# A gated delta-rule layer with experts: weights loaded in parts, biases added on VectorE, and sums of squares taken by ScalarE from transposed tiles

## The chip, the cores and the metric

The kernel runs on one core of a Trainium2 chip. The metric is the device time of one execution in microseconds (us), lower is better. A core has TensorE (PE; its weight loads are PEld), VectorE (DVE), ScalarE (ACT), GpSimd (POOL) and SyncE (SP), which issues the DMAs. Each engine runs its own instructions in the order in which the program gives them; semaphores join the engines.

## The reference, cut to what matters

Two batches of 2048 tokens with 256 features pass a gated delta-rule attention with a short convolution, and then a layer of one shared and 16 routed experts. The sums of squares in question are those of `_l2norm`; the biases in question are `bz`, `bb` and `ba`.

```python
mixed = hidden_states @ Wqkv.T + bqkv
z = hidden_states @ Wz.T + bz
beta = sigmoid(hidden_states @ Wb.T + bb)
a = hidden_states @ Wa.T + ba
g = -exp(A_log) * softplus(a + dt_bias)
mixed = silu(causal_conv4(mixed))              # then split into q, k (8 heads), v (16 heads)
q = _l2norm(q) * DK ** (-0.5);  k = _l2norm(k) # x * rsqrt(sum(x*x) + 1e-6)
# per token: state = state*exp(g); delta = (v - k.state)*beta; state += k delta; out = q.state
core = out * rsqrt(mean(out*out) + 1e-6) * norm_w * silu(z)
x = x + layernorm(core @ Wout.T + bout)
# then x = x + layernorm(shared expert + routed experts of layernorm(x))
```

## The kernel before, in words

The tokens are cut into 32 chunks of 128. The 16 value heads of a chunk are four groups, and one item `(t, g)` is one group of one chunk: 128 items. The recurrence within a chunk is solved by blocks: a triangular matrix is inverted, in part by GpSimd (16x16 blocks) and in part by matmuls.

Work is pipelined over items. When item `w` is in its state stage (`s`), item `w+1` (called `v`) is inverted (`i`), item `w+2` (`f`) is in its front stage, item `w+3` (`a`) is projected, and the output of item `w-1` (`u`) is projected (`p`). Between them stand the experts of the chunk before (`e`) and the norm and gates of the chunk after (`c`). Every engine has one function `item(w, stages)` in which this order is written out by hand, and `run` calls it for a few items ahead of the loop (the prologue), for the loop over chunks 1 to 30 (`Fori`, four items in one pass), and behind it. Nothing reorders the instructions.

The steps that the change and the prediction touch:

- **Loads.** SyncE issues the broadcast rows, then all weights, and every engine waits for all of them (`loaded`). VectorE then prepares constants: it scales `Wout` by `norm_w` (L1069), and splits `bz` and `bb, ba` into three bf16 parts each (L1077 to L1084), so that a bf16 matmul can add them.
- **Projection.** `proj` (PE L450) makes the q, k and v channels of item `a` as 128x128 tiles in the banks bF0 and bF1, with channels on partitions. ACT applies the last convolution tap (L810), VectorE the other three (L1101), and `activated` runs Silu to QK, Gz and VT. Two table loads (L793) stand around the Silus.
- **Gate.** `z_proj` adds `bz` by a bf16 matmul of 512 columns (L459), then makes z (L460, L462) in bF1. ACT takes Silu from the bank straight to Gz (L831). `chunk_front("ba")` has such a bias matmul too (L630).
- **Sums of squares.** ACT squares QK as one 128x512 instruction (L826, at the end of `activated`); `ss` has PE multiply each of the four squared tiles with a column of ones (L477), because channels lie on partitions; VectorE adds epsilon (`squares`, L1136), and ACT makes the logarithm and the inverse scale (`key_norm`, L844). `ktr` transposes the two k tiles (L484) into the bank bXT, which `ss` used too, and so waits for L1136. GpSimd's `exponents` (from L1444) starts at the logarithm and makes Parts, which `parts_t` transposes (L490).
- **Front and state.** `kkq` (L469) makes the products of keys and queries; `correct` (L565) and `refined` (DVE L1151) finish the inverse Tt; `right_side` (DVE L1158) and `solve` (L587) use it.

## Time and profile before

| | |
|---|---|
| median of three runs | 3621.46 us (3620.43 to 3624.41) |
| the profiled execution | 3620.91 us, of which the span is 3619.1 us |
| PE | 3296.9 us busy, 91% |
| DVE | 2712.9 us, 75% |
| ACT | 2441.7 us, 67% |
| POOL | 2162.0 us, 60% |
| mean granted clock of TensorE | 0.966 of full speed |

The busy shares are averages over the whole span, in which the first 68 us and the last 100 us look unlike the rest. Matmuls overlap, so the duration of one is longer than the distance from one to the next: where the text speaks of what a matmul costs, it means the distance between starts. A float32 matmul of the program appears as two records, a transpose as one. Records of some matmuls are missing in the loop (those of L459 and L502, for instance); a gap called "issue" of some 0.2 us stands in their place.

### The profile page before, as it was taken

To read this page: it belongs to the slowest core of one execution; us is meant where nothing else is said; L and a number is where in the kernel's file an instruction comes from. 1 tells how busy PE (TensorE), PEld (TensorE's weight loads), DVE (VectorE), ACT (ScalarE), POOL (GpSimd) and SP (SyncE) were. 2 spreads that over 40 slices of the span, in tenths; PEclk is the share of its full clock that TensorE was granted. 3 is DMA by queue.
4 is the path that set the end of the run, shared out by engine and by line. 5 is a ranking of instruction groups with operands and counts; after the bars stand their busy time and mean duration, and the time that the engine had idled before them with its cause. 6 is when DMAs were issued, how large, how long until landed. Compare 5 with 4: busy or idle time off the path is not lost.

```text
span 3619.1 us, 86991 instructions
## 1 busy us (share of the span) xinstructions
PE 3296.9 (91%) x24003; PEld 2944.1 (81%) x24256; DVE 2712.9 (75%) x8608; ACT 2441.7 (67%) x5922; POOL 2162.0 (60%) x5380
## 2 busy tenths in 40 slices
PE   1799999999999999999999999999999999999986
PEld 1688888888888888888888888888888888888875
DVE  3577787777787877777877778777777877777763
ACT  1576777767777667677677676676676667676662
POOL 0676666666666666666666666666566666566660
PEclk9899999999999999999999999999999999999996
DMA  3111111111111111111111111111111111111110
GB/s 156 37 43 34 41 35 35 41 38 33 41 34 35 43 35 34 43 32 41 38 35 41 36 32 42 36 35 40 36 32 40 38 35 40 37 32 42 36 40 4
DMA packets 423099, 142.70 MB, mean 39 GB/s; under 512 B 211120, under 2 KB 421616, under 8 KB 422128
## 3 DMA queue, kind: packets, MB, share of 16 engines
q1 hardware_dynamic: 422768, 139.83, 14.9%
q14 instruction: 312, 2.56, 0.2%
q8 instruction: 19, 0.31, 0.0%
HBM read 93.11 MB, written 46.66 MB: 39 GB/s over the span
## 4 chain that ended last, share of the span: by engine, by line
PE 66%; DVE 10%; ACT 10%; issue 9%; DMA 1%; POOL 1%; SPq 1%; DVEq 0%; ACTq 0%; POOLq 0%
PE bF L450 9%; PE bB L617 6%; PE bQ L530 5%; PE bXT L538 5%; PE bS L587 4%; PE bS L595 3%; PE bB L674 3%; ACT L793 3%; PE bB L668 3%; PE bS L579 2%; PE bD L602 2%; PE bQ L469 2%; PE bX L543 2%; PE bXT L477 2%; PE bD L580 2%
## 5 line engine op out<-in xcount | busy, mean ns | idle before, releaser
L1101 DVE SCALAR_TENSOR_TENSOR Y<-bF,Cv,Y 128x127 f32<-128x127 f32 (+2 forms) x3072 | 851.3, 338 | 18.0 <-ACT Y L810 13.2
L881 ACT ACTIVATE XiT<-bXT 128x512 fp32r<-128x512 f32 x384 | 229.5, 598 | 534.0 <-PE bXT L538 534.0
L450 PE MATMUL bF<-XnT,Wqkv 128*128 128x128 f32 x4096 | 549.0, 284 | 0.0
L450 PEld LDWEIGHTS bF<-XnT,Wqkv 128*128 128x128 f32 x4096 | 521.2, 200 | 7.0 <-issue 1.7
L810 ACT ACTIVATE Y<-bF,Cv 128x128 f32<-128x128 f32 x1024 | 385.2, 461 | 83.5 <-PE bF L450 83.5
L1517 POOL TENSOR_TENSOR Tp<-Tp 32x64 f32<-32x64 f32 (+2 forms) x768 | 359.8, 468 | 60.2
L1144 DVE TENSOR_TENSOR Qi<-bQ,Cf 128x512 fp32r<-128x512 f32 x384 | 265.0, 690 | 127.3 <-PE bQ L530 126.9
L793 ACT ACT_TABLE_LOAD x257 | 329.7, 1283 | 5.3 <-PEq L1601 0.7
L1510 POOL TENSOR_TENSOR Tp<-Cb,Yb 32x64 f32<-32x64 f32 (+1 forms) x384 | 275.5, 717 | 32.7 <-POOL Yb L1519 4.9
L1510 POOL TENSOR_TENSOR Tp<-Yb,Tm 32x64 f32<-32x64 f32 (+1 forms) x384 | 274.7, 715 | 30.1
L1411 POOL TENSOR_TENSOR Ln<-Ex,KKQ 128x512 f32<-128x512 f32 x128 | 164.2, 1283 | 207.5 <-ACT Ex L872 132.1
L538 PE MATMUL bXT<-Qi,Xi 128*128 128x128 f32 x1536 | 266.2, 296 | 7.3 <-DVE Qi L1144 7.0
L1525 POOL TENSOR_TENSOR Yb<-Cb,Cf 32x8 fp32r<-32x8 f32 x128 | 25.8, 202 | 406.6 <-DMA Cb<-DL 406.6
L538 PEld LDWEIGHTS bXT<-Qi,Xi 128*128 128x128 f32 x1536 | 212.6, 192 | 49.3 <-DVE Qi L1144 39.6
L617 PE MATMUL bB<-Wout,CoT 128*128 128x256 f32 x1024 | 250.3, 388 | 1.6 <-ACT Rl L957 0.8
L530 PE MATMUL bQ<-XiT,LnR 128*128 128x128 f32 x1536 | 234.1, 275 | 16.1 <-ACT XiT L881 16.1
L530 PEld LDWEIGHTS bQ<-XiT,LnR 128*128 128x128 f32 x1536 | 212.1, 191 | 36.9 <-ACT XiT L881 25.5
L888 ACT ACTIVATE Xi<-bX 128x512 fp32r<-128x512 f32 x384 | 225.8, 588 | 1.8 <-PE bX L543 0.3
L1444 POOL TENSOR_TENSOR HG<-LnbG,Lnk 128x4 f32<-128x4 f32 x128 | 30.1, 235 | 323.4 <-ACT Lnk L844 323.4
L1158 DVE SCALAR_TENSOR_TENSOR R<-bS,Sc,Vs 128x128 f32<-128x128 f32 x512 | 153.5, 340 | 80.6 <-issue 79.5
L617 PEld LDWEIGHTS bB<-Wout,CoT 128*128 128x128 f32 x1024 | 185.9, 192 | 22.3 <-ACT CoT L917 1.1
L587 PE MATMUL bS<-R,Tt 128*128 128x128 f32 x1024 | 176.2, 297 | 15.4 <-DVE Tt L1151 15.4
(217 smaller groups left out, 9335.2 us busy)
## 6 DMA issues: line engine op xcount, KB each, us to landing
DL<-Ln SPq DMA_DIRECT2D x128, 256.0 KB, 2.3
XiT<-DX SPq DMA_DIRECT2D x128, 256.0 KB, 2.9
Xi<-DX SPq DMA_DIRECT2D x128, 256.0 KB, 3.3
DX<-Yb SPq DMA_DIRECT2D x256, 32.0 KB, 1.9
Xf<-x SPq DMA_DIRECT2D x32, 128.0 KB, 2.8
Wqkv<-wqkv SPq DMA_DIRECT2D x1, 4096.0 KB, 15.8
Cb<-DL SPq DMA_DIRECT2D x128, 32.0 KB, 1.9
Xr<-x SPq DMA_DIRECT2D x32, 128.0 KB, 2.9
```

Source lines behind the costliest of these rows:

```text
L450: last = mm(bank[:, i, :], Wqkv[:, k, c:c + P], XnT[:, k, :], start=(k == 0), stop=(k == KT - 1))
L530: last = mm(heads(bQ)[:, h, :], LnR[:, h, :], XiT[:, h, :], start=True, stop=True)
L538: last = mm(heads(bXT)[:, h, :], Xi[:, h, :], Qi[:, h, :], start=False, stop=True, skip_group_check=True)
L587: last = mm(heads(bS)[:, i, :], Tt[:, 2 * p + i, :], R[:, i, :], start=True, stop=True)
L617: last = mm(bB[:, 0:HID], CoT[:, h, :], Wout[:, g * GH + h, :], start=(h == 0), stop=(h == GH - 1))
L793: nc.scalar.add_instruction(mybir.InstLoadActFuncSet(name=nc.get_next_instruction_name(), act_func_set_id=TABLES[name], engine=mybir.Engin ...
L810: last = op(Y[:, tile, :], bank[:, i, :], ACT.Identity, scale=c[:, TAPS - 1:TAPS], bias=c[:, TAPS:TAPS + 1])
L881: op(XiT[:, :, :], heads(bXT), ACT.Copy).then_inc(sem["xt_done"], 1)
L1101: last = stt(y, bank[:, i, 0:P - shift], Cv[:, g * TILES + tile, n:n + 1], y, ALU.mult, ALU.add)
L1144: tt(Qi[:, :, :], heads(bQ), level, ALU.mult).then_inc(sem["q_done"], 1)
L1510: then(tt(view(Tp[:, :], p * m ** 3, [[m * m, m], [m, m], [1, m]]), pair(left, p), pair(right, p), ALU.mult))
L1517: then(tt(lo, lo, hi, ALU.add))
```

## The change

It has three parts, and the written-out order of all engines' items is new as well.

- **Loads.** What the first item needs (tokens, constants, convolution weights, the gates' weights) is loaded first and has a semaphore of its own, as has the first quarter of Wqkv, its other three quarters, and Wz with the bias row of z. The rest is waited for at the first output projection. Wout is scaled in the first `gated`.
- **Biases.** The bf16 splitting and the two bias matmuls are gone. VectorE adds `bz` while it moves z from the bank to Gz (`gate_bias`, 128x512), and ACT runs Silu on Gz in place. VectorE adds `bb, ba` in the copy that it made anyway.
- **Sums of squares.** `ss` and the 128x512 square are gone. `ktr` transposes all four tiles, q and k, so that tokens lie on partitions. ACT squares each transposed tile from bXT (four instructions of 128x128) with the accumulator output, which gives the sums in Ssq.

```diff
-        LOADS = [(whole(d), src) for d, src in (
-            (Xf, x[0]), (Cf, constf), (Wqkv, wqkv), (Cv, conv), (Norm, cols), (Wba, wba), (Wz, wz), (Wout, wout),
-            (Sh1, shared1), (Wlat, wlat), (Sh2, shared2), (Rw, rw), (Rw2, rw2))]
+        EARLY = [(whole(d), src) for d, src in ((Xf, x[0]), (Cf, constf), (Cv, conv), (Wba, wba))]
+        EARLY += [(Gz[:, :, :, :].rearrange("p a b c -> p (a b c)")[:, 0:14 * P], consth)]
+        LOADS = [(whole(d), src) for d, src in (
+            (Norm, cols), (Wout, wout), (Sh1, shared1), (Wlat, wlat), (Sh2, shared2), (Rw, rw), (Rw2, rw2))]
...
+            for g in range(GROUPS):
+                c = slice(g * TILES * P, (g + 1) * TILES * P)
+                sp.dma_start(Wqkv[:, :, c], wqkv[:, :, c]).then_inc(qkv_in if g else first_in, 16)
+                if g == 0:
+                    sp.dma_start(Wz[:, :, :], wz).then_inc(z_in, 16)
+                    sp.dma_start(Zf[:, :], rows[0:1, 0:HV * P].to_broadcast([P, HV * P])).then_inc(z_in, 16)
...
             def z_proj(f, part):
-                    mm(bF1[:, :], onesb, Zb[:, c], start=True, stop=False)
-                    mm(bF1[:, :], XnT[:, 0, :], Wz[:, 0, c], start=False, stop=False)
+                    mm(bF1[:, :], XnT[:, 0, :], Wz[:, 0, c], start=True, stop=False)
...
-            def ss(f):
-                pe.wait_ge(sem["xt_done"], at("xt_done", ahead(f, -2)))
-                pe.wait_ge(sem["sq_done"], at("sq_done", f))
-                for i in range(2 * GK):
-                    last = mm(bXT[:, i:i + 1], Sq[:, i, :], ones[:, 0:1], start=True, stop=True)
-                last.then_inc(sem["ss_full"], 1)
...
             def ktr(f):
-                pe.wait_ge(sem["sse_done"], at("sse_done", f))
-                for kh in range(GK):
-                    last = nc.tensor.transpose(heads(bXT)[:, kh, :], QK[:, g, 2 * kh + 1, :], ident)
+                pe.wait_ge(sem["xt_done"], at("xt_done", ahead(f, -2)))
+                pe.wait_ge(sem["silu_done"], at("silu_done", f, 1))
+                for i in range(2 * GK):
+                    last = nc.tensor.transpose(heads(bXT)[:, i, :], QK[:, g, i, :], ident)
...
             def parts_t(f):
+                pe.wait_ge(sem["sq_done"], at("sq_done", f))
...
             def square_qk(f):
-                act.wait_ge(sem["silu_done"], at("silu_done", f, 1))
-                act.wait_ge(sem["ss_full"], at("ss_full", ahead(f, -1)))
-                op(Sq[:, :, :], QK[:, f[1], :, :], ACT.Square).then_inc(sem["sq_done"], 1)
+                act.wait_ge(sem["ktr_full"], at("ktr_full", f))
+                act.wait_ge(sem["sse_done"], at("sse_done", ahead(f, -1)))
+                for i in range(2 * GK):
+                    last = op(Sq[:, i, :], heads(bXT)[:, i, :], ACT.Square, accum_out=Ssq[:, i:i + 1])
+                last.then_inc(sem["sq_done"], 1)
...
             def gate(f):
-                act.wait_ge(sem["z_full"], at("z_full", f))
-                op(Gz[:, f[1], :, :], heads(bF1), ACT.Silu).then_inc(sem["gz_done"], 1)
+                act.wait_ge(sem["zb_done"], at("zb_done", f))
+                op(Gz[:, f[1], :, :], Gz[:, f[1], :, :], ACT.Silu).then_inc(sem["gz_done"], 1)
...
             def squares(f):
-                dve.wait_ge(sem["ss_full"], at("ss_full", f))
+                dve.wait_ge(sem["sq_done"], at("sq_done", f))
                 dve.wait_ge(sem["lnk_done"], at("lnk_done", ahead(f, -1)))
-                ts(Sse[:, :], bXT[:, 0:2 * GK], L2_EPS, None, ALU.add).then_inc(sem["sse_done"], 1)
+                ts(Sse[:, :], Ssq[:, :], L2_EPS, None, ALU.add).then_inc(sem["sse_done"], 1)
...
+            def gate_bias(f):
+                dve.wait_ge(sem["z_full"], at("z_full", f))
+                dve.wait_ge(sem["core_done"], at("core_done", ahead(f, -GROUPS)))
+                tt(Gz[:, g, :, :].rearrange("p a b -> p (a b)"), bF1[:, :], Zf[:, g * GH * P:(g + 1) * GH * P], ALU.add)\
+                    .then_inc(sem["zb_done"], 1)
...
             def gated(w):
+                if isinstance(w[0], int) and w == (0, 0):
+                    dve.wait_ge(loaded, 16 * len(LOADS))
+                    ts(Wout[:, :, :], Wout[:, :, :], Norm[:, 0:1], None, ALU.mult).then_inc(wout_done, 1)
```

How the order moves is shown at three places. The first is PE at the start of an item in the loop, from the projection to `solve` (L587 before, L598 in the changed kernel). Before:

```order
L450 MATMUL bF<-XnT,Wqkv 128x128 x8
L474 ISA
L475 ISA
L477 MATMUL bXT<-Cf,Sq 128x1 x4
L563 REGISTER_ALU
L565 MATMUL bX<-Xi,Qi 128x128 x4
L467 ISA
L469 MATMUL bQ<-QK 128x256 x2
L484 MATMUL bXT<-Cf,QK 128x128 x2
L584 REGISTER_ALU
L585 REGISTER_ALU
L587 MATMUL bS<-R,Tt 128x128 x2
```

In the changed kernel, at the same place of PE (`kkq`, now L485, stands just ahead of the first row):

```order
L491 ISA
L494 MATMUL bXT<-Cf,QK 128x128 x4
L449 REGISTER_ALU
L453 ISA
L454 REGISTER_ALU
L465 MATMUL bF<-XnT,Wqkv 128x128 x8
L576 MATMUL bX<-Xi,Qi 128x128 x4
L456 ISA
L465 MATMUL bF<-XnT,Wqkv 128x128 x8
L595 REGISTER_ALU
L596 REGISTER_ALU
L598 MATMUL bS<-R,Tt 128x128 x2
```

The four multiplications with ones are gone, the transposes are four and come ahead of the projection, and the whole projection (8 and 8 tiles) stands ahead of `solve`, with only `correct` (L576) between its halves.

The second place is ACT at the end of item g=0 in the loop, from the copy of the normalized tokens (XnT) on. Before:

```order
L930 ACTIVATE XnT<-bB 128x256
L793 ACT_TABLE_LOAD
L816 REGISTER_ALU
L817 ACTIVATE QK<-Y 128x512
L831 ACTIVATE Gz<-bF 128x512
L821 ACTIVATE VT<-Y 128x512
L793 ACT_TABLE_LOAD
L826 ACTIVATE Sq<-QK 128x512
L909 REGISTER_ALU
L910 ACTIVATE Vl<-Vv 128x4
L912 ACTIVATE Fr<-Vl 128x4
L888 ACTIVATE Xi<-bX 128x512
```

In the changed kernel, at the same place of ACT:

```order
L939 ACTIVATE XnT<-bB 128x256
L931 ACTIVATE Ve<-Ve 128x1
L933 ACTIVATE Ve<-Ve 128x1
L802 ACT_TABLE_LOAD
L825 REGISTER_ALU
L826 ACTIVATE QK<-Y 128x512
L841 ACTIVATE Gz<-Gz 128x512
L830 ACTIVATE VT<-Y 128x512
L802 ACT_TABLE_LOAD
L918 REGISTER_ALU
L919 ACTIVATE Vl<-Vv 128x4
L921 ACTIVATE Fr<-Vl 128x4
```

The square Sq is gone from the row, and the two small instructions on Ve (the inverse deviation of the third norm, `norm2`), which stood behind Xi, now stand ahead of the table load. Behind Fr follow two instructions on Ab (`chunk_front("ba")`), and then Xi.

The third place is DVE at the start of a loop pass (item g=0). Before:

```order
L1158 SCALAR_TENSOR_TENSOR R<-bS,Sc,Vs 128x128 x2
L1106 REGISTER_ALU
L1107 ISA
L1107 TENSOR_SCALAR Bk<-Cv,Cf 128x8
L1134 ISA
L1135 REGISTER_ALU
L1136 TENSOR_SCALAR Sse<-bXT 128x4
L1138 TENSOR_SCALAR Epq<-Sse 128x2
L1149 REGISTER_ALU
L1150 ISA
L1151 COPY Tt<-bX 128x512
```

In the changed kernel, at the start of the same pass on DVE (Tt, now L1157, follows the last row):

```order
L1104 TENSOR_SCALAR Bk<-Cv,Cf 128x8
L1196 ISA
L1199 SCALAR_TENSOR_TENSOR O<-O,Fr,Gz 128x128 x4
L1131 ISA
L1132 REGISTER_ALU
L1133 TENSOR_SCALAR Sse<-Ssq 128x4
L1135 TENSOR_SCALAR Epq<-Sse 128x2
L1161 REGISTER_ALU
L1164 SCALAR_TENSOR_TENSOR R<-bS,Sc,Vs 128x128 x2
L1127 TENSOR_TENSOR KKQ<-bQ,Cf 128x512
L1155 REGISTER_ALU
L1156 ISA
```

The four instructions of `gated` (O) and `products` (KKQ) moved ahead of Tt, and R moved behind Sse.

## Rows read from the trace of the kernel before

**Rows 1.** The page, busy time of each engine.
```profile
PE 3296.9 (91%) x24003; PEld 2944.1 (81%) x24256; DVE 2712.9 (75%) x8608; ACT 2441.7 (67%) x5922; POOL 2162.0 (60%) x5380
```

**Rows 2.** Busy by windows: window, length, PE, PEld, DVE, ACT, POOL, clock, DMA.
```profile
20.00:40.00 20.00, 0.00 (x0) 0.00 (x0) 0.00 (x0) 0.00 (x0) 0.00 (x0) 1.00 0.99 415
...
1000.00:2000.00 1000.00, 944.06 (x6961) 845.80 (x7035) 781.89 (x2498) 706.74 (x1723) 628.36 (x1567) 0.98 0.15 37
...
1843.66:1871.95 28.29, 24.65 (x164) 21.52 (x164) 21.63 (x70) 18.29 (x48) 15.02 (x42) 0.94 0.17 42
```

**Rows 3.** PE's waits from 1000 to 2000 us: total, times, longest.
```profile
PE bXT L484 <- DVE Sse L1136: 18.1, 9, 2.1
```

**Rows 4.** Timeline of PE: start, length, what, idle before; g=0 begins at 1843.66.
```profile
1798.53 0.61 PE L595 MATMUL bS<-Z,AT 128*128 128x128 f32 x4
...
1844.52 1.95 PE L450 MATMUL bF<-XnT,Wqkv 128*128 128x128 f32 x16
1846.31 0.95 PE L477 MATMUL bXT<-Cf,Sq 128*128 128x1 f32 x8
1847.12 0.64 PE L565 MATMUL bX<-Xi,Qi 128*128 128x128 f32 x4
1847.60 1.08 PE L469 MATMUL bQ<-QK 128*128 128x256 f32 x4
1850.58 0.44 PE L484 MATMUL bXT<-Cf,QK 128*128 128x128 f32 x2 [1.91 <-DVE Sse L1136]
1851.58 0.71 PE L587 MATMUL bS<-R,Tt 128*128 128x128 f32 x4 [0.56 <-DVE Tt L1151]
...
1854.06 1.06 PE L595 MATMUL bS<-Z,AT 128*128 128x128 f32 x4
```

**Rows 5.** Timeline of DVE, start of the same item.
```profile
1846.67 0.42 DVE L1301 TENSOR_TENSOR Yo<-Yo,X 128x256 f32<-128x256 f32 x1
1849.72 0.61 DVE L1158 SCALAR_TENSOR_TENSOR R<-bS,Sc,Vs 128x128 f32<-128x128 f32 x2 [2.62 <-issue]
...
1851.36 1.14 DVE L1190 SCALAR_TENSOR_TENSOR O<-O,Fr,Gz 128x128 f32<-128x128 f32 x4
```

**Rows 6.** Timeline of all engines, the prologue.
```profile
14.99 0.22 ACT L798 ACTIVATE Rows<-Rows 128x16 f32<-128x16 f32 x1 [12.96 <-DMA Rows<-rows]
...
44.50 0.21 DVE L1059 TENSOR_SCALAR Tails<-Cv 128x96 f32<-128x96 f32 x1 [39.87 <-DMA Gz<-consth]
...
47.41 2.35 DVE L1069 TENSOR_SCALAR Wout<-Wout,Norm 128x4096 f32<-128x4096 f32 x1
...
66.18 0.43 DVE L1201 BATCH_NORM_STATS2 St<-Xf 128x6 f32<-128x256 f32 x1
...
68.28 0.66 PE L625 MATMUL bB<-Cf,Xn 128*128 128x128 f32 x2 [68.28 <-DVE Xn L1216]
```

**Rows 7.** The chain that ended last, pieces of one item: start, length, what.
```profile
1796.69 0.22 PE bXT L484 x2
...
1800.25 0.22 PE bQ L506
```

**Rows 8.** Groups by line and form: busy, mean ns of one, idle before.
```profile
L810 ACT ACTIVATE Y<-bF,Cv 128x128 f32<-128x128 f32 x1024 | 385.2, 461 | 83.5 <-PE bF L450 83.5
...
L900 ACT ACTIVATE Z<-bS 128x256 f32<-128x256 f32 x256 | 98.5, 385 | 55.9 <-PE bS L587 55.5
...
L1283 DVE TENSOR_TENSOR Rl<-bF,Rl 128x512 f32<-128x512 f32 x128 | 87.4, 683 | 39.2 <-ACT Rl L959 39.2
...
L826 ACT ACTIVATE Sq<-QK 128x512 f32<-128x512 f32 x128 | 80.6, 630 | 1.4
```

**Rows 9.** Timeline of ACT, end of item g=0 (PE starts g=1 at 1871.95).
```profile
1869.53 1.28 ACT L793 ACT_TABLE_LOAD   x1
```

**Rows 10.** Timeline of DVE, the norms in item g=0.
```profile
1868.88 1.53 DVE L1244 TENSOR_TENSOR X<-X,Xr 128x256 f32<-128x256 f32 x1
...
1871.13 0.15 DVE L1206 TENSOR_SCALAR Ve<-Mv 128x1 f32<-128x1 f32 x1
```

More of the change, by code:

```diff
@@ L365, in _ @@
             sp.sem_inc(stored, 16)
-            sp.dma_start(Vs[:, :, :, :].rearrange("p a b c -> p (a b c)"),
-                         rows[0:1, 0:HV * P].to_broadcast([P, HV * P])).then_inc(rows_in, 16)
+            for dst, src in EARLY:
+                sp.dma_start(dst, src).then_inc(early, 16)
             sp.dma_start(BabS[:, 0:2, :].rearrange("p a b -> p (a b)"),
@@ L692, in item @@
                     experts(t - 1, "D", 0)
+                if front:
+                    kkq(f)
+                    ktr(f)
                 if new:
@@ L695, in item @@
                     proj(a, 0, 1)
-                if front:
-                    ss(f)
                 if state:
                     correct(w)
-                if front:
-                    kkq(f)
-                    ktr(f)
+                if new:
+                    proj(a, 1, 0)
+                    proj(a, 1, 1)
                 if state:
                     solve(w, 0)
-                if e and g == 3:
-                    experts(t - 1, "D", 2)
-                if new:
-                    proj(a, 1, 0)
+                if front:
+                    parts_t(f)
+                    vtr(f)
+                    exponents(f)
                 if post:
@@ L734, in item @@
                     invert_xt(v, 0)
+                if e and g == 1:
+                    experts(t - 1, "ffn1", 0)
+                if invert:
+                    invert_x(v, 0)
+                if e and g == 2:
+                    experts(t - 1, "G", 1, a if new else (chunks - 1, GROUPS - 1))
                 if e and g == 3:
                     experts(t - 1, "G", 3, a if new else (chunks - 1, GROUPS - 1))
[L737 to L738 removed]
+                if state:
+                    solve(w, 1)
                 if invert:
[L740 removed]
                     invert_q(v, 1)
@@ L1306, in item @@
                 new, front, invert, state, post, e, c = [s in stages for s in "afispec"]
+                if new:
+                    ended(a)
                 if c and g == 1:
                     chunk_front(t + 1, "ba")
-                if state:
-                    right_side(w, 0)
-                if new:
-                    ended(a)
+                if e and g == 2:
+                    experts(t - 1, "D", 0)
+                if post:
+                    gated(u)
                 if front:
```

285 lines of the change are left out of this document (137 added, 148 removed).

## The prediction, made before the changed kernel ran

> **What bounds the kernel now.** I read the busy shares first: PE is busy for 91% of the span, DVE for 75% and ACT for 67% [rows 1]. The windows then divide the span. Between 20 and 40 us no engine works and the DMAs move 415 GB/s; in the thousand microseconds from 1000 on, PE is busy for 944 at a clock of 0.98, DVE for 782, ACT for 707 [rows 2]. So the loop is bound by PE's own stream, and the start by loading and setup. PE's waits say what the other 56 us are: the largest is `ktr` behind VectorE's Sse, 18.1 us in 9 waits, once in each loop pass of four items [rows 3]. The timelines show why. The pass ends on DVE with Yo, the next DVE instruction starts 2.62 us later with nothing that it waited for (the jump back of the loop), and PE stands for 1.91 us at L484 and 0.56 us at L587 [rows 4, 5]. Behind that stop the matmuls run at half speed for a while (1.06 us for a group that takes 0.61 us elsewhere), and the window of this item has a mean granted clock of 0.94 [rows 2, 4]: full speed is 2.4 GHz, and the level behind the stop is 1.2 GHz.
>
> **The start.** Before, DVE begins its setup at 44.50 us, when the last of all loads is in, and PE starts at 68.28 us [rows 6]. DVE's Wout scaling (2.35 us) and nearly everything between its end and the first norm instruction at 66.18 us (the bf16 splitting) leave the setup. Now five tensors come first, 1.7 MB. At the 415 GB/s of [rows 2] these are 4.1 us; the row for A_log landed by 14.99 us with 1.7 MB queued around it [rows 6], so I put the end of the early loads at 16.5 us. Of the DVE setup 3.0 us of small instructions remain, then the 2.1 us from that norm instruction to PE (68.28). PE starts at about 21.8 us, 46.4 us sooner. The first quarter of Wqkv (1 MB, 2.5 us more) is in by then. Wz, the bias row and the rest of Wqkv end near 33 us, and PE wants z 16 us after its start, at 38 us: covered. If that cover went, PE would wait a few us once. The Wout scaling comes back, once, in `gated`: 2.35 us. Net 44 us; bounds 36 (a late quarter of weights, and a slower fill of the pipeline, because `kkq` now stands ahead of the next projection) and 50.
>
> **PE's stream in an item.** Removed: `ss`, 0.81 us from its start to that of the next group [rows 4], and the bias matmul of z, which has the form of L506: 0.22 us [rows 7]. Added: two more transposes, 0.22 us by the row of the two that are there [rows 7]. Net 0.81 us in each of 128 items: 104 us. The small bias matmul once in a chunk is under 0.1 us and I leave it at nothing. If PE stayed as closely packed as now, the loop would give all of it.
>
> **What is added elsewhere.** DVE gets `gate_bias`, 0.68 us by the equal form of L1283 [rows 8]: 87 us, which DVE, idle for 218 of 1000 us, can hold, except in item g=0 where the loop jump has cost it 2.62 us. ACT loses a square of 0.63 us and gets four of 128x128. No row shows the accumulator output. From below, the 385 ns of a 128x256 copy from a bank say about 0.2 us each in a row; from above, I take 1.0 us each, which is more than twice any row of that width (L810: 461 ns, four in 1.51 us). I take 0.35 us, near L810: 1.4 us for four.
>
> Here the Trainium skill, "ScalarE: Activation LUTs", section "What ACT_TABLE_LOAD costs", gives 186 ns plus 0.833 ns per element for an ACTIVATE with immediates, with an overlap of 93 ns back to back; its price for four squares would be 0.9 us, an estimate, and its 399 ns for 256 elements agrees with L900's 385 ns. It gives no price for reading out the accumulator. By it the four squares would end 0.5 us sooner and the sum would come out some 15 to 30 us lower.
>
> The place of these squares matters more than their sum. Before, squaring was done in the tail of the previous item and the sums came after the projection. Now the chain ktr, four squares, Sse, then R, KKQ and Tt on DVE lies ahead of `solve`, with two projection halves and `correct` on PE to hide it (1.79 us for 8 tiles and 0.48 for `correct`, by the distances between starts in [rows 4]; 1.79 + 0.48 + 1.79 = 4.1 us). DVE stands at Sse with R, KKQ, Tt and the taps queued behind it; ACT stands at the squares with Qg, the logarithm and Y behind them; POOL waits for the logarithm, and PE for POOL's Parts at L501, about 2.0 us after it. I walk through the four items of a pass.
>
> - g=2 and g=3: an expert step of 0.8 us on PE stands ahead. ktr ends 3.1 us into the item, ACT is free at 3.0 and 3.6, the sums are there at 4.7 and 5.3, Tt at 6.4 and 7.0; PE is ready at 7.1. Parts arrive at about 7.3 and 7.9 where PE wants them at 7.5. Given back: 0.1 and 0.3 us.
> - g=0: DVE's jump still ends at 1849.72 by the times of [rows 5]. Behind it come Bk, `gated` (1.14), Sse, R, KKQ and Tt: ready at 1853.3, where PE is ready at 1849.9. So the stop moves from ktr to `solve`: 3.4 us instead of 2.5, but the whole projection is already behind it. The clock falls as before. Of the 0.9 us of longer stop I count 0.3, between 0 and 0.9: a PE that arrives later waits less for DVE in the rest of the item.
> - g=1: the instructions on Ve for `norm2` now stand ahead of the table load on ACT. Their input is DVE's last statistic, at 1871.13 before, after an add of 1.53 us [rows 10]; the table load stood at 1869.53 [rows 9]. By my walk that statistic comes at about 1870.7, so Silu, the second table load and Xi move 1.6 us later, less the 0.53 us of the square that is gone. PE would wait 0.65 us at `kkq`, 0.5 at `correct`, 1.1 at `solve`, 0.3 at Parts: 2.5 us. Each of them rests on differences of half a microsecond, so the bounds are 0 and 2.5 and I take the middle, 1.2.
>
> Together 1.9 us in a pass, times 31: 59 us given back of 104.
>
> **Sum**, against the profiled execution's 3620.9 us (0.5 under the median, so they are one): 3620.9 - 44 - 104 + 59 = 3532 us.
>
> A rule speaks against the change: the Trainium skill, "ScalarE: Activation LUTs", section "Rules for kernel authors", says to put multiplications and additions on VectorE and not on ScalarE, up to three times faster in bf16. In float32 this trace has 630 ns for a 128x512 square on ACT and 683 ns for a product on DVE [rows 8], so the rule has nothing to gain here, and DVE is the busier engine.
>
> **The rivals.**
> - **A, nothing is given back** (chance 0.25). For it: ACT and DVE have idle time in every item, and the waits that I find are small. Against: both engines now hold a longer serial chain at the head of the item. 3620.9 - 44 - 104 = 3473 us.
> - **B, the loop gains nothing** (0.20). Each item waits as long as its stream got shorter, because the chain over squares, Sse and Tt ends last instead of PE. For it: the upper end of my walk in g=1, and DVE in g=0 with 21.6 us of work in 28.3 [rows 2], a jump of 2.6 and 0.7 more. Against: g=2 and g=3. 3620.9 - 44 = 3577 us.
> - **C, slower** (0.06). The squares with accumulator take 1.0 us each, so that Sse, the logarithm, Parts and Tt come 2.6 us later in all 128 items. The 0.1 to 0.4 us of slack at `solve` and Parts take little of it: about 2.3 us of new wait in an item, 294 us. 3620.9 - 44 - 104 + 294 = 3767 us. It decides above a new wait of 1.15 us in an item (148 / 128), or squares of about 0.7 us each. ACT would still be under 90% busy; only the chain tells.
> - **D, the start gives less** (0.03): a DMA of the early ones lands late because sixteen engines serve all queued loads at once, and PE starts at 40 us: 3620.9 - 28 - 104 + 59 = 3548 us, inside my range.
>
> **How the numbers follow.** The forecast has 0.46, A 0.25, B 0.20, C 0.06, D 0.03. The time is the forecast's, 3532 us, with a range of its own of 3495 to 3565. The range for 8 in 10 reaches down nearly to A's sum with the upper bound of the start, and up beyond B: 3460 to 3600. A measurement of this kernel tells 0.2%, 7 us, from no change. All cases but C are faster by more; between them and C I leave 0.02 for the same: faster 0.92, same 0.02, slower 0.06.
>
> **What would show it.** Right: PE's first matmul near 22 us; no L477 rows, L494 x4 at 0.43 us; PE's largest wait at L598 behind Tt, once in a pass and about 3.4 us, with DVE's jump before it; in g=1 waits at L485 and L598 of 0.5 to 1 us; the squares at 0.3 to 0.4 us apart. Wrong: squares over 0.7 us apart (C); waits of PE under 50 us in a thousand (A); a wait for Parts or Tt in all four items (B); PE's start after 30 us (D).

## The result, and the profile of the changed kernel

The changed kernel takes 3665.66 us (median of 4 runs, 3662.04 to 3668.66) against 3620.94 us for the kernel before in the same comparison: a ratio of 1.0122, 95% interval 1.0105 to 1.014. It is slower. The forecast was 3532 us and faster, with a range of 3460 to 3600.

The page of the changed kernel, its head, PE's clock and the two queues that carry instructions (packets, MB, share):

```profile
span 3666.9 us, 86575 instructions
PE 3259.1 (89%) x23200; PEld 2807.8 (77%) x23328; DVE 2841.8 (77%) x8720; ACT 2502.0 (68%) x6818; POOL 2149.4 (59%) x5380
...
PEclk8999999999999999999999999999999999999996
...
q8 instruction: 279, 4.57, 0.5%
q14 instruction: 313, 2.56, 0.3%
```

Beside [rows 1], PE has less work (3259 against 3297 us; the records of 128 matmuls are missing here and those of 253 there, so that the two can't be compared closely) and DVE more (2842 against 2713). Queue q8 has 279 packets of 16 KB; the page of the kernel before has 19, and 312 for q14. Where the time went shows in an instruction that runs once in every chunk, the weight load of the transpose of La (kernel before, then changed; the two times are the first and the last start):

```profile
L678 PEld LDWEIGHTS bB<-Cf,La x32: 137/138/183, 332.0 to 3611.6; 128*128 128x128 f32 x32
```
```profile
L691 PEld LDWEIGHTS bB<-Cf,La x32: 138/138/183, 287.8 to 3659.3; 128*128 128x128 f32 x32
```

The start gives 44.2 us. The 31 chunks between take 3279.6 us before and 3371.5 after: 105.8 and 108.8 us each. The loop loses 92 us, the start gives 44, and the difference is the 48 us of the spans. Below, "a pass" is always this figure, last start minus first, divided by 31. It is some 2 us less than four items in the middle of the loop take, because the last two of the 31, behind the loop, lack stages: they take 95 and 52 us.

PE's waits from 1000 to 2000 us (total, times, longest), of the changed kernel:

```profile
PE bS L590 <- issue: 42.6, 9, 5.3
PE bB L687 <- DVE Rl L1292: 11.1, 9, 2.0
PE bS L598 <- DVE Tt L1157: 7.1, 10, 0.7
...
PE bQ L485 <- DVE Qi L1143: 4.7, 9, 0.5
```

The wait of [rows 3] is gone, as forecast. The stop of 3.4 us that the forecast put at L598 is not there (0.7 us). Instead PE stops for 4.7 us at L590, the first matmul of the pass, and no semaphore is to blame for it. PE, DVE and ACT around it, at the same place as [rows 4, 5]:

```profile
1849.23 0.48 PE L569 MATMUL bQ<-XiT,NegR 128*128 128x512 f32 x1
1854.45 1.01 PE L590 MATMUL bS<-S,QK 128*128 128x256 f32 x2 [4.74 <-issue]
1855.26 1.06 PE L591 MATMUL bD<-S,QK 128*128 128x256 f32 x2
1856.11 1.91 PE L485 MATMUL bQ<-QK 128*128 128x256 f32 x4
1857.82 1.06 PE L494 MATMUL bXT<-Cf,QK 128*128 128x128 f32 x4
```
```profile
1855.76 0.23 DVE L1104 TENSOR_SCALAR Bk<-Cv,Cf 128x8 f32<-128x8 f32 x1 [2.77 <-issue]
1855.95 1.14 DVE L1199 SCALAR_TENSOR_TENSOR O<-O,Fr,Gz 128x128 f32<-128x128 f32 x4
1860.26 0.17 DVE L1133 TENSOR_SCALAR Sse<-Ssq 128x4 f32<-128x4 f32 x1 [3.17 <-ACT Sq L836]
```
```profile
1858.99 0.28 ACT L836 ACTIVATE Sq<-bXT 128x128 f32<-128x128 f32 x1 [6.55 <-PE bXT L494]
1859.17 0.19 ACT L836 ACTIVATION_READ_ACCUMULATOR Sq<-bXT 128x1 f32 x1
1859.26 0.27 ACT L836 ACTIVATE Sq<-bXT 128x128 f32<-128x128 f32 x1
```
```profile
1850.00:1854.00 4.00, 0.00 (x0) 0.19 (x1) 1.41 (x3) 2.37 (x6) 1.50 (x5) 0.88 0.13 19
1854.00:1858.00 4.00, 3.55 (x9) 2.73 (x9) 1.32 (x5) 0.00 (x0) 0.00 (x0) 0.50 0.10 14
```

Before the change PE went from one pass to the next without a stop [rows 4]. Now it stands for 4.7 us, ACT and DVE stand behind it, and the matmuls after it run at 1.2 GHz: in the last two rows (windows: PE, PEld, DVE, ACT and POOL busy, then the granted clock) the clock is 0.50 for the four microseconds behind the stop. DVE's own stop at the jump is there as before, now covered. The squares are cheap: 0.25 us from one to the next in the median, with a readout of 0.2 us between them that is an instruction of its own.

### The profile page after: what moved, and what is told of

Its sections match the earlier page's. It is cut to its first block, busy times and chain, and to the rows that moved or that the text cites. A ratio compares the mean times of both kernels' runs of the same rounds, so it can differ in the third digit from the quotient of the medians.

```text
span 3666.9 us, 86575 instructions
## 1 busy us (share of the span) xinstructions
PE 3259.1 (89%) x23200; PEld 2807.8 (77%) x23328; DVE 2841.8 (77%) x8720; ACT 2502.0 (68%) x6818; POOL 2149.4 (59%) x5380
## 4 chain that ended last, share of the span: by engine, by line
PE 63%; DVE 13%; issue 10%; ACT 9%; DMA 2%; POOL 2%; SPq 0%; DVEq 0%; POOLq 0%; ACTq 0%
PE bF L465 9%; PE bB L631 5%; DVE Y L1098 4%; PE bXT L549 4%; PE bS L590 3%; PE bS L598 3%; PE bQ L541 3%; PE bB L687 3%; PE bF L478 3%; PE bB L681 3%; PE bQ L485 3%; PE bD L591 2%; PE bF L476 2%; PE bS L606 2%; ACT L802 2%
## 5 line engine op out<-in xcount | busy, mean ns | idle before, releaser
L1098 DVE SCALAR_TENSOR_TENSOR Y<-bF,Cv,Y 128x127 f32<-128x127 f32 (+2 forms) x3072 | 854.3, 340 | 43.2 <-ACT Y L819 29.9
L465 PE MATMUL bF<-XnT,Wqkv 128*128 128x128 f32 x4096 | 515.8, 280 | 0.0
L465 PEld LDWEIGHTS bF<-XnT,Wqkv 128*128 128x128 f32 x4096 | 490.5, 196 | 0.0
L549 PE MATMUL bXT<-Qi,Xi 128*128 128x128 f32 x1536 | 283.5, 307 | 27.0 <-DVE Qi L1141 23.1
L590 PE MATMUL bS<-S,QK 128*128 128x256 f32 x512 | 177.1, 430 | 141.7 <-issue 140.6
L1522 POOL TENSOR_TENSOR Tp<-Cb,Yb 32x64 f32<-32x64 f32 (+1 forms) x384 | 276.0, 719 | 32.6 <-POOL Yb L1531 4.6
L836 ACT ACTIVATE Sq<-bXT 128x128 f32<-128x128 f32 x512 | 134.2, 280 | 211.2 <-PE bXT L494 211.2
L1199 DVE SCALAR_TENSOR_TENSOR O<-O,Fr,Gz 128x128 f32<-128x128 f32 x512 | 171.1, 395 | 55.2 <-ACT Fr L921 54.9
```

Of the source, the lines that this page charges most:

```text
L465: last = mm(bank[:, i, :], Wqkv[:, k, c:c + P], XnT[:, k, :], start=(k == 0), stop=(k == KT - 1))
L549: last = mm(heads(bXT)[:, h, :], Xi[:, h, :], Qi[:, h, :], start=False, stop=True, skip_group_check=True)
L590: mm(bS[:, 0:2 * P], QK[:, g, 2 * p + 1, :], s, start=True, stop=True).then_inc(sem["ks_full"], 1)
L1098: last = stt(y, bank[:, i, 0:P - shift], Cv[:, g * TILES + tile, n:n + 1], y, ALU.mult, ALU.add)
L1522: then(tt(view(Tp[:, :], p * m ** 3, [[m * m, m], [m, m], [1, m]]), pair(left, p), pair(right, p), ALU.mult))
```

## The experiments

A pass has four items, g=0 to 3. In the table an item is the time from one start of the single NegR matmul (L558 before, L569 after) to the next, median of 8 to 11 passes between 1500 and 2600 us. Each time is the median of four runs (ten for e18), and each ratio is to runs of the kernel before on the same chip.

| kernel | time us | ratio to before (95%) | a pass | g0 | g1 | g2 | g3 |
|---|---|---|---|---|---|---|---|
| before | 3620.9 | 1 | 105.8 | 28.3 | 26.8 | 26.0 | 26.9 |
| changed | 3665.7 | 1.0105 to 1.014 | 108.8 | 29.7 | 29.1 | 25.2 | 27.1 |
| e1, changed, shifted 110 | 3632.2 | 1.0026 to 1.0059 | 107.5 | 27.4 | 31.5 | 25.2 | 27.1 |
| e2, before, shifted 150 | 3588.7 | 0.990 to 0.9933 | 104.6 | 27.0 | 26.8 | 26.0 | 26.9 |
| e3, changed, shifted 30 | 3641.5 | 1.0048 to 1.0081 | 107.8 | 27.5 | 31.5 | 25.2 | 27.1 |
| e4, before, written out | 3481.9 | 0.9594 to 0.9626 | 101.5 | 23.6 | 26.5 | 26.0 | 27.0 |
| e5, changed, written out | 3519.6 | 0.9696 to 0.9744 | 103.7 | 23.5 | 29.9 | 25.2 | 27.1 |
| e6, e1 with mask_q early | 3929.1 | 1.0831 to 1.087 | 116.8 | 30.4 | 30.8 | 27.4 | 30.9 |
| e7, e5 in the old order | 3589.8 | 0.9922 to 0.9956 | 105.7 | 24.2 | 29.0 | 27.2 | 27.6 |
| e8, e5, proj ahead in g1 | 3505.6 | 0.9683 to 0.9731 | 103.5 | 23.4 | 29.7 | 25.2 | 27.0 |
| e9, e5, mask_q early in g0 | 3513.3 | 0.9709 to 0.9746 | 103.5 | 23.5 | 30.2 | 25.2 | 27.0 |
| e10, e5 without gate bias | 3494.9 | 0.9628 to 0.968 | 103.1 | 23.4 | 29.8 | 25.2 | 27.2 |
| e11, old order, bias on DVE alone | 3523.5 | 0.9714 to 0.9764 | 103.7 | 23.4 | 28.7 | 26.5 | 27.2 |
| e12, old order, squares alone | 3537.4 | 0.9745 to 0.9795 | 104.2 | 24.2 | 27.7 | 26.8 | 27.5 |
| e13, e4 with the new start | 3454.6 | 0.9535 to 0.9568 | 101.5 | 23.6 | 26.6 | 26.2 | 27.0 |
| e14, e5, first_tokens late | 3457.0 | 0.955 to 0.9586 | 101.8 | 22.6 | 28.6 | 25.2 | 27.0 |
| e15, e4 without ss matmuls | 3456.3 | 0.9537 to 0.9574 | 100.6 | 23.6 | 26.2 | 25.7 | 26.9 |
| e16, changed, first_tokens late | 3678.0 | 1.0141 to 1.02 | 109.0 | 30.9 | 28.9 | 25.2 | 27.1 |
| e17, e14 and e8 together | 3464.9 | 0.9558 to 0.9613 | 102.1 | 22.6 | 28.5 | 25.2 | 27.0 |
| e18, e1, first_tokens late | 3611.0 | 0.9964 to 0.9987 | 106.8 | 26.9 | 29.2 | 25.2 | 27.1 |

The kernel before took 3612 to 3621 us in these comparisons, so a difference of less than some 8 us between rows of different comparisons says nothing; where it matters, the difference by the ratios (times 3621 us) stands beside that of the times. Items and passes are those of one profiled execution. That of e4 was 9 us above e4's median, so its 101.5 us a pass is 0.3 too high, and what is slower than e4 by its pass is slower by as much more. e15's was 7 us above its own, so those two compare well. e10, e12 and e15 compute something else than the reference, as their expectations say; all others compute the same.

**Is it the jump back? (e1, e3, e2)** PE gets repeated waits on a count that it has long passed, ahead of its program. They cost it nothing in the loop, but they shift where the loop's body lies in PE's program: the 220 waits of e1 add 110 instructions (by the pages' counts, PE's matmuls left out), the 60 of e3 add 30 and the 300 of e2 add 150.

```
+            for _ in range(220):          # 60 in e3, 300 in e2 (kernel before)
+                pe.wait_ge(setup, 1)
             pe.wait_ge(setup, SETUP)
```

> The changed kernel with 110 more instructions in front of PE's loop (waits for a semaphore value that is long there, executed while PE waits for the loads anyway). Nothing else moves. Theory J: the stop of 4.74 us at the start of each pass on PE is a fetch of instructions. Counted in blocks of 256 instructions (16 KB, the size of the packets on queue q8), the loop body now starts at instruction 1726 and ends at 3342, which touches 8 blocks; before it was 1812 to 3476, 7 blocks, and q8 moved nothing in the loop. With 110 more it is 1836 to 3452, 7 blocks. J expects: q8 falls from 279 packets to about 20, the stop at L590 goes, DVE's own stop of 2.8 us stays and makes PE wait at solve (L598) for about 3 us in place of it, and the time falls by 3 to 6 us a pass, to 3485 to 3580 us. Rival O (the new order itself: PE's last waits of a pass, for LaT and for Ln, hold up the jump): nothing changes, 3660 to 3670 us, 279 packets. Rival C (the chain over the squares costs the time in all items): nothing changes either.

> A placebo for the shift of 110: the changed kernel with 30 more such instructions on PE. The loop body is 1756..3372, still 8 blocks of 256. Theory J: no change, 3655 to 3675 us, about 279 packets on q8 and the stop at L590 as in the changed kernel. A theory by which any additional instruction or the time at which PE starts matters expects a change here as with 110.

> The kernel before with 150 more such instructions in front of PE's loop, executed while PE waits 68 us for the loads. The loop body moves from 1812..3476 (7 blocks of 256) to 1962..3626 (8 blocks). Theory J: q8 now moves about 9 packets in each of 29 jumps (some 280 in all), PE stops for 3 to 5 us at L579 at the start of each pass, and the time grows by 60 to 200 us, to 3680 to 3820 us, though no useful instruction is added. Rivals O and C: 3615 to 3627 us, 19 packets.

PE's waits (1000 to 2000 us) and the row of queue q8 in the page, of e1 and then of e2:

```profile
PE bS L598 <- DVE Tt L1159: 30.5, 12, 3.3
PE bQ L485 <- DVE Qi L1145: 13.1, 9, 1.9
```
```profile
q8 instruction: 19, 0.31, 0.0%
```
```profile
PE bS L579 <- issue: 10.9, 9, 1.5
PE bF L450 <- issue: 10.8, 9, 1.4
```
```profile
q8 instruction: 281, 4.60, 0.5%
```

In e1 q8 is back to 19 packets and the stop at L590 is gone. The changed kernel moves some 9 packets more in each jump (260 more in 29 jumps), and of the pass shown above one of them moves from 1848.9 to 1849.8 us and the next from 1851.9 to 1853.0, the second within PE's stop. So PE stands there for the fetching of its own instructions, and whether it has to depends on where the body lies. My rule for where is refuted: e3 was meant as a placebo with as many blocks as the changed kernel, and it has 18 packets, no stop at L590, and is 24 us faster. What decides it stays open.

The 3.4 us at L598 that the prediction named are there now (3.3 at most). But the gain is 33 us (29 by the ratios), not the 85 or more that I expected. The table shows where the rest is: g0 gives 2.3 us and g1 takes 2.4 back, in which PE now stands 1.5 us a pass at L485 where the changed kernel stands 0.5. It seems that the stop at the jump had let DVE catch up. e2 refutes the price that I put on it: with as many packets as the changed kernel the kernel before gets faster by 31 us. There the stop comes in two pieces of 1.2 us each, PE's wait of 2 us for Sse is gone, since Sse is ready when PE asks for it, and the mean clock is 0.982 against 0.966. Fetching costs what it displaces, and the clock behind it.

**No jump at all (e4, e5), and e6.** The loop over the chunks is written out, for all engines.

```
-            with eng.Fori(1, chunks - 1) as t:
+            for t in range(1, chunks - 1):
```

> The kernel before with its loop over the chunks written out, so that no engine ever jumps back; the instructions and their order are the same. Theory J (part of the loss comes from the stops of PE and DVE at the jump, and the low clock behind them): item g0 falls from about 27.9 us to the 26.6 us that it takes in the kernel before shifted by 150, the others stay (26.4, 26.0, 26.9), the clock is 0.98 or more, DVE's R has no stop of 3 us, and the time is 3565 to 3595 us. Rival (code that runs through never comes from a buffer, so that the fetch itself is the limit): every engine stops here and there all along, and the time is above 3650 us.

> The changed kernel with its loop written out. Theory J: PE's stop at L590, DVE's stop at Bk and the wait of PE at L598 for Tt (3.2 us) all go. From the items of the changed kernel shifted by 110 (27.4, 29.2 to 31.6, 25.2, 27.1 us), g0 gives up 3.2 us and the slow matmuls behind it: 23.9, 27 to 29, 25.2, 27.1, so 103 to 105 us a pass against 106 in the written-out kernel before: 3480 to 3560 us, faster than that by 30 to 90 us. Rival O (the new order is worse by itself, above all kkq and ktr right behind ks_qs in item g1): PE's wait at L485 stays at 1.9 us with its low clock, g1 stays near 29 us, and the kernel is not faster than the written-out kernel before (3570 to 3620 us).

> The changed kernel shifted by 110, with DVE's mask_q(v, 3), the last operation of its item, moved ahead of gate_bias, out_norm and the last expert steps. Theory O (in item g1 PE stands at L485 for 1.9 us behind this Qi, then runs 6 us at the low clock): Qi comes 1.6 us earlier, the wait falls below 0.6 us, no low clock follows it, g1 falls from 29.2 us to 26 to 27, and the time from 3632 us to 3540 to 3590 us. Rival S (what ends that wait is ACT's QK, 1856.4 us, or the wait only moves to L549 or L598 of the same item): under 0.7 us a pass, 3610 to 3635 us.

The jump costs both kernels far more than I thought, 139 and 146 us, and nearly the same: it is not what sets them apart. e4 is below its whole expected range. In the kernel before g0 alone pays for it, 28.3 to 23.6 us. What remains is a changed kernel that is 2.2 us a pass slower with no jump in it. The time of e5 lies in theory J's range, but it has the signs of rival O: the wait at L485 stays, g1 takes 30 us, and it is not faster than e4. g2 has the forecast 0.8 us; g0 and g1 together take 53.4 us against 50.1, where PE's shorter stream alone would have made them 1.6 less. In g1 PE stands 1.9 us at L485 and then runs at 1.2 GHz for most of four microseconds (the timeline's row, and the window whose clock is 0.57):

```profile
1806.51 2.08 PE L485 MATMUL bQ<-QK 128*128 128x256 f32 x4 [1.86 <-DVE Qi L1143]
```
```profile
1806.00:1810.00 4.00, 3.49 (x13) 3.02 (x14) 2.10 (x8) 3.39 (x12) 0.95 (x3) 0.57 0.20 23
```

g3 gives nothing either. PE's largest waits in e5 (1000 to 2000 us) have two that e4 has at 1.1 us (behind Qi) or hardly at all (behind Rl); the one at L687 falls in g3, 0.9 us in each pass, and takes back what PE saves there:

```profile
PE bQ L485 <- DVE Qi L1143: 14.2, 9, 1.9
PE bXT L549 <- DVE Qi L1141: 10.3, 19, 1.0
PE bB L687 <- DVE Rl L1292: 9.2, 10, 2.0
```

e6 moves the Qi that ends the wait at L485 on DVE, `mask_q(v, 3)`, ahead of `gate_bias` and `out_norm` in all items:

```
+                if invert:
+                    mask_q(v, 3)
                 if new:
                     gate_bias(a)
```

Neither theory held; it is 297 us slower than e1. DVE now stands at Qi for PE's L569, 26 times in some 34 items, with everything queued behind it:

```profile
DVE Qi L1145 <- PE bQ L569: 80.6, 26, 4.4
```

**Is it that wait? (e8, e9)** In e8 the two projections go ahead of kkq and ktr on PE in g1; in e9 Qi goes ahead of `gate_bias` on DVE in g0 alone.

```
+                if new and g == 1:            # e8, PE
+                    proj(a, 0, 0); proj(a, 0, 1)
                 if front:
                     kkq(f)
                     ktr(f)
```

```
                 if state:                     # e9, DVE: end of the item
                     update_s(w, 1)
                 ...
+                if invert and g == 0:
+                    mask_q(v, 3)
                 if new:
                     gate_bias(a)
```

> The changed kernel written out, and in item g1 alone proj(a, 0, 0) and (a, 0, 1) stand ahead of kkq and ktr on PE, as before the change. Theory O (the stop of 1.9 us at L485 and the 4 us at the low clock behind it are most of the loss): both go, g1 falls from 29.9 to 31.2 us to 26 to 27, 3520 - 31 x (3 to 4.5) = 3380 to 3430 us. Rival M (the stop only moves on, to L598 behind Tt of the same item, since ktr and so ACT's squares come later): g1 gains less than 1 us, 3490 to 3520 us.

> The changed kernel written out, with DVE's mask_q(v, 3) ahead of gate_bias and out_norm in item g0 alone, where PE has long written what it reads. Theory O: Qi comes 1.3 to 1.6 us earlier, the wait at L485 in g1 falls from 1.9 us to about 0.6 (ACT's QK ends it then), no low clock follows, g1 falls by 1.2 to 3 us: 3430 to 3485 us. Rival H (DVE stands behind PE there as in the kernel with the same move in all four items, which lost 10 us a pass): g0 grows, 3530 us or more.

No: 14 and 6 us by the times, 5 and nothing by the ratios, which is no more than the noise between chips. In e8 the 1.9 us and the low clock are gone, and PE stands instead at L576 for Xi (9.1 us in a thousand) and at L598 for Tt (6.2): rival M has it. In e9 the wait is down to 0.8 us, now for ACT's QK, the granted clock in g1 is full, and g1 takes 30.2 us all the same, while g0 does not grow: neither theory held. The wait was the sign of an engine that is late, not the cause.

**Order or operations? (e7, e10, e11, e12)** e7 has the changed operations in the item order before; e11 undoes in it the sums of squares, e12 the gate's bias; e10 undoes the gate's bias in the new order.

```
-                    ss(f)                     # e7, PE, in the order before
+                    ktr(f)
...
-                op(Gz[:, f[1], :, :], Gz[:, f[1], :, :], ACT.Silu)
+                op(Gz[:, f[1], :, :], heads(bF1), ACT.Silu)          # e10, e12, ACT
...
-                if new:                       # e10, e12, DVE
-                    gate_bias(a)
...
-                    ktr(f)                    # e11, PE; squares, keys and Sse as before
+                    ss(f)
```

> The changed operations and loads in the order of the kernel before, loop written out: ktr stands where ss stood, ACT's squares behind its first tap, DVE's squares behind refined and gate_bias ahead of out_norm. Theory O (the operations are worth what was predicted, the new order lost it): from the items of the written-out kernel before (23.6, 26.5, 26.0, 27.0 us for g0 to g3) each gives up about the 0.8 us that item g2 gained in the written-out changed kernel (25.2), and the start 44 us: 3482 - 44 - 31 x 3.2 = 3340 us, with 3330 to 3400. Rival S (the 0.7 us that DVE has more per item for the gate's bias and the 0.5 us that ACT has more for squares and their readouts are on the path, whatever the order): only the start is gained, 3430 to 3480 us.

> The changed kernel written out, with the gate's bias left out altogether (no add on DVE, no matmul on PE; ACT takes the SiLU from PSUM): the kernel computes the gate without its bias. Theory D (from the middle of item g0 to the middle of g1 DVE has no idle time, so what the change gave it there, first the add of 0.69 us, is on the path): at least the adds of g0 and g1 come back, 1.4 us a pass, and up to all four, 2.7 us: 3520 - 31 x (1.4 to 2.7) = 3436 to 3477 us. Rival W (DVE's load is no bound; PE's waits in g1 come from the order of PE's own work): under 0.5 us a pass, 3505 to 3525 us.

> The order before, written out, with the new loads and the biases added on DVE, but the sums of squares as before (one square, eight one-column matmuls). The written-out kernel before takes 3482 us and the start gives 44, so 3438 us with nothing else. With the squares undone against the kernel with all changed operations in the old order (3590 us): theory S (ACT's four squares with their readouts and the chain through ktr, squares and gated are what lost 4.9 us a pass there): 3438 to 3460 us. Theory D (DVE's adds lost it): 3550 us or more.

> The order before, written out, with the new loads and the new sums of squares, and the gate's bias left out altogether (the kernel computes the gate without its bias). Theory S (the new squares lose most of it in this order): 3550 us or more, since core_t waits behind gated, gated behind squares, and squares behind ACT's last readout, 0.8 to 1.2 us in each item. Theory D (the adds on DVE lost it): 3345 to 3440 us.

Against e4's 101.5 us a pass: the bias alone 2.2 us more, the squares alone 2.7 us more, both 4.2 us. So each edit loses by itself and the new order wins two of the four back. e7 is above both of its ranges, and e11 and e12 lie between theirs: each part is a cause. PE's waits, of e12 and of e11:

```profile
PE bB L620 <- DVE O L1195: 24.0, 28, 0.9
PE bB L620 <- DVE Dp L1292: 9.6, 10, 1.0
```
```profile
PE bXT L493 <- ACT Sq L844: 16.1, 24, 0.8
```

Read together with the order in which each engine holds its work, they say this. With the squares, `core_t` waits on PE for DVE's gated O, which is queued behind Sse, and that behind ACT's last readout. With the bias, ACT's SiLU of the gate waits for DVE, and the square behind it, and PE for the square. e10 is 25 us faster than e5, less than theory D asked for and more than rival W allowed. It is rather a lower bound of what DVE's add costs in the new order, since in e10 PE gets the bank back only when ACT has read it.

**What is PE's work worth? (e15)** Only the 8 one-column matmuls leave the kernel before, written out.

```
-                    ss(f)
...
-                ts(Sse[:, :], bXT[:, 0:2 * GK], L2_EPS, None, ALU.add)
+                ts(Sse[:, :].unsqueeze(2), Sq[:, :, 0:1], 1000.0, None, ALU.add)
```

> The kernel before written out, with the 8 one-column matmuls per item left out: DVE takes the first column of the squares plus a constant in place of their sums, so q and k are scaled by wrong norms; all else stands. Forecast's term (PE's stream sets the pace, and 1.0 us less of it per item shortens each item by 0.8 to 1.0 us): 3482 - 31 x (3.2 to 4) = 3358 to 3383 us. Rival W (PE's busy share hides waits: what follows waits for ACT or DVE anyway): under 1.5 us a pass, 3435 to 3482 us.

The rows of those matmuls in e4 (count, busy, mean ns, idle before), and PE's largest wait in e15:

```profile
L477 PE MATMUL bXT<-Cf,Sq 128*128 128x1 f32 x312 | 37.8, 242 | 5.0 <-ACT Sq L826 5.0
```
```profile
PE bX L559 <- ACT Xi L880: 24.6, 38, 1.2
```

PE has 3.2 us a pass less to do by the distances between starts (0.81 us in each item; 3.9 us by the busy time, 37.8 us in 9.7 passes), and the pass is 0.9 us shorter; the time is 26 us less (20 by the ratios). Rival W holds. The rest comes back at L559, the next group: it waits for ACT's Xi, 0.65 us each time, in every item. The removed matmuls had filled that gap.

**Why is DVE late in g0 and g1? (e14, e16, e18)** In e5 DVE is not idle for more than 0.05 us at a time between 1889 and 1913.9 us, that is from 3 us into an item g0 to 4.6 us into g1. DVE and POOL there (start, duration):

```profile
1897.03 1.29 POOL L1423 TENSOR_TENSOR AT<-Ex,KKQ 128x512 f32<-128x512 f32 x1
1897.07 1.27 DVE L1122 TENSOR_TENSOR Y<-Y,Hd 128x12 f32<-128x12 f32 x1
...
1906.34 1.50 POOL L1522 TENSOR_TENSOR Tp<-Cb,Yb 32x512 f32<-32x512 f32 x1
1906.47 1.53 DVE L1250 TENSOR_SCALAR X<-Acc,Mv,Ve 128x256 f32<-128x256 f32 x1
...
1909.62 1.48 POOL L1522 TENSOR_TENSOR Tp<-Yb,Tm 32x512 f32<-32x512 f32 x1
...
1910.30 0.96 DVE L1259 TENSOR_SCALAR Hn<-X,Mv,Ve 128x256 f32<-128x256 f32 x1
```

An addition of 12 columns takes 0.16 us where it runs free and 1.27 us here, and each of the three DVE rows ends 0.0 to 0.2 us after the POOL row that it overlaps. This is no accident of one place: of the 256 such additions in e5 66 last over 0.6 us, and each of these ends 24 to 38 ns after a POOL instruction beside it, while the 126 in e14 that have no POOL instruction beside them take 157 to 171 ns. The Trainium skill, "SBUF — State Buffer", section "SBUF: two separate sides", says that a DVE instruction with two SBUF inputs and a GpSimd instruction that reads SBUF take a shared port pair in turn, the first for its whole length. The first pair of rows agrees. The other two DVE instructions have one such input and two columns of scalars; the section names two-port modes as well, and no run here tests those. e14 moves that addition on DVE:

```
-                if new:
-                    first_tokens(a, 0)
                 if invert:
                     mask_q(v, 0)
                 ...
                 if state:
                     right_side(w, 1)
+                if new:
+                    first_tokens(a, 0)
```

> The changed kernel written out, with DVE's first_tokens(a, 0) moved behind mask_q(v, 0) and right_side(w, 1). Theory P (this small DVE operation, 0.16 us where it runs free, lasts up to 1.3 us because POOL's 1.29 us operation runs beside it, and in g0 and g1 DVE's time is on the path): its mean falls from 0.43 us to below 0.25 us, DVE's busy time by 1 to 1.5 us a pass, and the time by 15 to 45 us, to 3475 to 3505 us. Rival W (DVE's stretched operations are off the path): its mean falls and the time stays at 3515 to 3525 us.

The instruction's group in e5 and e14:

```profile
L1122 DVE TENSOR_TENSOR Y<-Y,Hd 128x12 f32<-128x12 f32 x75 | 32.0, 427 | 0.0
```
```profile
L1122 DVE TENSOR_TENSOR Y<-Y,Hd 128x12 f32<-128x12 f32 x78 | 17.9, 230 | 0.0
```

Theory P holds and with more than it asked for: one small move gives 63 us (55 by the ratios), g0 0.9 and g1 1.3 us. The mean of X<-Acc, L1250, falls with it from 1142 to 401 ns. Does the same hold in the loop? e16 is that one move in the changed kernel, e18 in e1.

> The changed kernel itself, with its loop, and the one move on DVE: first_tokens(a, 0) behind mask_q(v, 0) and right_side(w, 1). Theory P (what the new order loses is in good part DVE's small operations lasting beside POOL's long ones; written out, the move gave 63 us): 3666 - (45 to 80) = 3586 to 3621 us, level with the kernel before or just below. Rival F (in the loop PE's stop at the jump, 4.7 us a pass, covers what DVE gains, since DVE catches up there): less than 20 us, 3645 to 3670 us.

> The changed kernel shifted by 110, so that PE fetches nothing at the jump (3632 us), with first_tokens(a, 0) late on DVE. If PE's stop at the jump is what covered the move in the changed kernel itself (3678 against 3666 us) and the move is worth here what it is written out (63 us): 3570 to 3600 us. If DVE's own stop at the jump, 2.8 us, covers it too: 3615 to 3640 us.

No. In the changed kernel itself the mean falls too (369 to 234 ns) but the time rises by 12 us (17 by the ratios); PE's stop at the jump grows from 4.7 to 6.1 us, and X<-Acc had nothing to give, since it takes 0.40 us in the changed kernel already:

```profile
PE bS L590 <- issue: 55.3, 9, 6.7
```

Without that stop (e18 against e1) the move gives 21 us, between the two ranges of e18. So PE's stop covers a part of what DVE gains, and probably DVE's own stop another. Why PE's stop grows in e16 is open.

**The start alone, and the two moves together (e13, e17).** e13 is e4 with the new loads and waits; the gate's bias stays a matmul, its row split on DVE once PE runs.

```
+                for dst, src in EARLY: ...    # e13: SP, and the waits of all engines, as changed
...
+                if isinstance(t, int) and w == (-1, 1):    # DVE
+                    gate_row()                # the splitting of the bias row into bf16
...
                     mm(bF1[:, :], onesb, Zb[:, c], start=True, stop=False)
```

e17 has the edits of e8 and e14.

> The kernel before written out, with the new order of the loads and waits at the start and the small bias added on DVE once per chunk, but the gate's bias as a matmul (its row is split after PE has begun) and the sums of squares as before. If the start is worth 44 us by itself and the rest of the time is the written-out kernel's (3482 us): 3435 to 3455 us, the fastest so far. If the start's gain is not additive (PE waits later for what was moved): 3460 to 3482 us.

> The changed kernel written out, with both moves: first_tokens late on DVE, and in item g1 proj(a, 0, 0) and (a, 0, 1) ahead of kkq and ktr on PE. With first_tokens late alone PE still stands 1.34 us a pass at L485 in g1. If that wait goes with its low clock as it did before (14 us there): 3457 - (14 to 45) = 3412 to 3443 us, the fastest. If it only moves to L598 and L576 of the same item: 3445 to 3465 us.

e13 is 4.5% below the kernel before, and no other correct kernel here is faster; e14 is level with it within the intervals. e13's start gives 27 us (21 by the ratios), its first transpose of La comes 32.6 us earlier than e4's, and a pass takes the same. That is less than the 44 us of the changed kernel, whose DVE has no row to split; that this is the reason was not tested. e17 adds nothing to e14: the wait at L485 goes and comes back at L598 and L576, as its second range had it.

## Why the prediction was wrong, point by point

- **The start, 44 us: right in the sum.** The first transpose of La comes 44.2 us earlier. The two terms were each off by about 2 us, in opposite directions: the first matmul starts at 23.57 us (forecast 21.8, from terms that add up to 21.6), and of the 2.35 us that I took off for the scaling of Wout hardly anything is seen.
- **The squares, 1.4 us for four: a little high.** They take 1.14 us with their readouts. Rival C asked for 1.0 us each; it was slower for none of its reasons.
- **PE's stream, 0.81 us less per item: this step failed.** "So the loop is bound by PE's own stream" and "If PE stayed as closely packed as now, the loop would give all of it" took PE's busy share as the bound. e15 measures it: 3.2 us a pass less for PE are worth 0.9, and of the 104 us some 25 were to be had. PE looked closely packed because its own work filled the gaps in which it would otherwise have waited; the place that tells is the chain behind each removed group, here PE's X for ACT's Xi, which I had not walked. Only g2 gave its 0.8 us in the changed order.
- **What is given back, 1.9 us a pass: too small, and of the wrong kind.** I walked the chain through the squares but put `gate_bias` into DVE's idle time. In the old order the bias alone costs 2.2 us a pass (e11) and the squares 2.7 (e12). In the new order it is DVE between g0 and g1: its work in the two items rose from 42.3 us in e4 to 46.5 in e5 (medians of ten passes), of which 1.4 us are the bias and 2.1 the additions of 12 columns, drawn out beside POOL. The prediction named [rows 10]'s add of 1.53 us and did not ask why it took that long. The answer was worth about half of what e5 missed (55 to 63 us of 113, by e14).
- **The jump: priced for DVE and not for PE.** I wrote that the stop "moves from ktr to `solve`", 3.4 us. It does in e1. In the changed kernel PE has a stop of its own ahead of it, 4.7 us, because its instructions are fetched again in each pass. Taking that away gives 33 us (e1).

In a sum: written out, the loop's forecast of -1.45 us a pass (-3.35 + 1.9) came out as +2.2, which is 113 us over 31 passes; the loop brings 108.8 - 105.8 = +3.0 instead of +2.2, 25 us more; the two make 138 us, and 3532 missed by 134. Rival B (the loop gains nothing) had the right reason in part, the chain over ACT and DVE ending last, and stopped at zero. What in the new order besides the drawn-out instructions costs g1 its last two microseconds (28.6 in e14 against 26.5, with the small matmul `ba` moved into it) was not taken apart further.

## What to carry to other kernels

An engine that is busy for 91% is not thereby the bound: take the group out and look which wait stands behind it, before counting its length as gain. A small instruction on VectorE is to be priced where it will stand, with what GpSimd does at that time, and by its own longest rows and not by its median. In a long loop written for five engines look at the jump first; here it was worth more than anything tried in the body, and writing it out took one line.

## What the runs showed of the hardware that I had not expected

- A jump back can make an engine fetch its instructions again: 9 packets of 16 KB on q8 and a stop of 4.7 us for PE. 60 waits ahead of the loop remove it (e3: 18 packets). With 300 of them in the kernel before the packets are there and the stop is two pieces of 1.2 us (e2). Written out, q8 has about 200 packets in all, and PE has no such stop.
- The jump costs the kernel before 139 us, 4.5 us a pass. What is seen of it there: DVE stands 2.7 us and POOL 2.1 us with nothing to wait for, PE waits 2.5 us behind them, and the granted clock of the item is 0.94. An estimate from that clock, 0.06 of 28.3 us, gives 1.7 us more for matmuls at 1.2 GHz.
- The same DVE addition takes 0.16 to 1.4 us by what POOL runs beside it.
- A squaring of 128x128 on ACT with its sum read out costs 0.25 us in a row: 0.28 us for the record of the operation and 0.21 for the readout, which overlap.
